# Twelve stack loads issued by ScalarE in place of SyncE, in a fused attention and mixture-of-experts kernel

## What is computed

```python
x = x + _L0_attn_ref(_layernorm(x), w_q, w_k, w_v, w_o)
x = x + _L0_ffn_ref(_layernorm(x), gate_w, w1, w2, w3)
# attention: scores = q k^T / sqrt(16); softmax over the keys; times v; times w_o
# experts: top 2 of softmax(x gate_w^T); silu(x w1^T) * (x w3^T), times w2, weighted and summed
```

## Time and profile before

| | before |
|---|---|
| time, median of 3 runs | 560.6 us (559.58 to 563.26) |
| the profiled execution's own time | 561.26 us |
| its span | 559.4 us |
| TensorE busy in the span | 539.2 us, 96% |
| VectorE busy | 386.4 us, 69% |
| ScalarE busy | 324.4 us, 58% |
| chain of work that ended last | TensorE 81%, VectorE 12%, issue 3% |
| granted TensorE clock, mean | 0.988 |

### The profile page before, as it was taken

One profiled execution on the slowest core, in us unless ns is written; L12 is line 12 of the kernel. 1 busy time (PEld: TensorE's weight loads), 2 busy tenths in 40 slices (PEclk: granted clock), 3 DMA queues, 4 the chain that ended last, 5 costly groups with the idle time before them and its releaser, 6 DMA issues.

```text
span 559.4 us, 9700 instructions
## 1 busy us (share of the span) xinstructions
PE 539.2 (96%) x3508; PEld 392.7 (70%) x3508; DVE 386.4 (69%) x706; ACT 324.4 (58%) x480; POOL 116.2 (21%) x145
## 2 busy tenths in 40 slices
PE   9999999899999999999999999999999999999991
PEld 6887664333333333333778979999999999999981
DVE  6915657889998999961688986755738375667650
ACT  5322116767878777878346463756657475757540
POOL 4300111002022020622001202334341321241212
PEclk9999999989999999999998999999999999999997
DMA  8290367937475753004463599593854757586112
GB/s 325 108 114 0 56 107 88 101 48 88 70 100 73 92 75 99 12 19 166 149 227 119 189 349 346 138 318 50 292 148 159 263 143 279 117 301 160 31 29 37
DMA packets 29068, 78.19 MB, mean 140 GB/s; under 512 B 7644, under 2 KB 8924, under 8 KB 24538
## 3 DMA queue, kind: packets, MB, share of 16 engines
q1 hardware_dynamic: 23722, 68.84, 46.9%
q0 software_dynamic: 5296, 8.69, 8.4%
HBM read 53.11 MB, written 9.32 MB: 112 GB/s over the span
## 4 chain that ended last, share of the span: by engine, by line
PE 81%; DVE 12%; issue 3%; ACT 1%; POOL 1%; DMA 0%; SPq 0%; POOLq 0%; DVEq 0%; ACTq 0%
PE ps L728 16%; PE ps L729 15%; PE ps L730 15%; PE ps_o L740 8%; DVE neg_max L1469 7%; PE ps L759 6%; PE ps L771 4%; PE ps_m L759 3%; PE ps L799 2%; PE ps_m L777 1%; DVE w_lo L1578 1%; PE ps_o L728 1%; PE ps_m L728 1%; PE ps_m L730 1%; PE ps_m L1026 1%
## 5 line engine op out<-in xcount | busy, mean ns | idle before, releaser
L1254 ACT ACTIVATE probs_t<-ps 128x1024 f32<-128x1024 f32 x128 | 124.1, 1021 | 33.2 <-PE ps L771 32.5
L1469 DVE TENSOR_REDUCE neg_max<-ps 128x1 f32<-128x512 f32 x170 | 111.2, 683 | 14.4 <-PE ps L759 10.8
L728 PE MATMUL ps<-xgT_hi,w_hi 128*128 128x256 f32 (+7 forms) x380 | 109.5, 288 | 1.0 <-DVE xgT_lo L1735 1.0
L729 PE MATMUL ps<-xgT_lo,w_hi 128*128 128x256 f32 (+7 forms) x380 | 108.5, 286 | 0.0
L730 PE MATMUL ps<-xgT_hi,w_lo 128*128 128x256 f32 (+7 forms) x380 | 108.5, 286 | 0.0
L728 PEld LDWEIGHTS ps<-xgT_hi,w_hi 128*128 128x128 f32 x380 | 72.0, 189 | 1.3 <-DVE xgT_lo L1735 1.1
L759 PE MATMUL ps<-k_stack,q_stack 48*128 48x512 f32 x170 | 69.3, 462 | 3.5 <-issue 1.7
L729 PEld LDWEIGHTS ps<-xgT_lo,w_hi 128*128 128x128 f32 x380 | 72.0, 189 | 0.1
L730 PEld LDWEIGHTS ps<-xgT_hi,w_lo 128*128 128x128 f32 x380 | 71.9, 189 | 0.0
L740 PE MATMUL ps_o<-probs_t,v_ones 128*32 128x512 f32 x512 | 68.8, 610 | 0.0
L1752 DVE TENSOR_TENSOR act<-gate,ps 128x256 f32<-128x256 f32 (+7 forms) x48 | 20.7, 430 | 66.8 <-PE ps L730 51.2
(11 more groups left out here) (329 smaller groups left out, 983.9 us busy)
## 6 DMA issues: line engine op xcount, KB each, us to landing
w_sb<-w SPq DMA_DIRECT2D x16, 1024.0 KB
w_sb<-w SPq DMA_DIRECT2D x8, 1536.0 KB
w_sb<-w SPq DMA_DIRECT2D x8, 1152.0 KB
q_stack<-q_hi SPq DMA_DIRECT2D x32, 128.0 KB, 5.2
k_stack<-k_hi SPq DMA_DIRECT2D x32, 128.0 KB, 4.9
q_stack<-q_lo SPq DMA_DIRECT2D x16, 128.0 KB, 4.5
k_stack<-k_lo SPq DMA_DIRECT2D x16, 128.0 KB, 5.9
q_hi<-o_raw SPq DMA_DIRECT2D x16, 128.0 KB, 5.1
```

Source lines behind the costliest of these rows:

```text
L728: pe.matmul(o, x_hi, w_hi, start=start, stop=False)
L729: pe.matmul(o, x_hi, w_lo, start=False, stop=False)
L1254: a.activation(probs_t[:, kc % 2, 2 * half:2 * half + 2, :], ps4[:, 2 * (n % 2):2 * (n % 2) + 2, :], ACT.Exp, scale=D ** -0.5).then_inc(s_ ...
L1469: v.tensor_reduce(neg_max[:, g % 2, col:col + 1], max_bank(g, u2), AX.X, ALU.max, negate=True).then_inc(s_mx, 1)
```

## The change: who issues the loads of pair 3, and when

`stack` now takes the engine that issues. SyncE no longer loads pair 3. ScalarE does, in its step (s, p) = (0, 2), after exponentials 2 and 3 of the first group and before exponentials 4 and 5. It waits for the same two semaphores first. The transfers, their sources, their targets and the semaphore that they raise are the same.

```diff
+        def stack(eng, pair, pars, kinds):
+
+            at = pair % RING
+            for par in pars:
+                for part, (qsrc, ksrc) in enumerate(((q_hi, k_hi), (q_lo, k_hi), (q_hi, k_lo))):
+                    dst = slice(HALF * par + D * part, HALF * par + D * (part + 1))
+                    for kind in kinds:
+                        to, frm = (qs, qsrc) if kind == "q" else (ks, ksrc)
+                        eng.dma_start(to[at][dst, :, :].bitcast(f32),
+                                      frm[HALF * par:HALF * (par + 1), pair, :].bitcast(f32)).then_inc(s_stack[at], 16)
...
-                elif s == 0:
-                    ready(3)
-                    stack(3, range(2), "qk")
...
+                if (s, p) == (0, 2):
+                    a.wait_ge(s_ones, RING)
+                    a.wait_ge(s_jd, d_count[n_of["k", 0, 3]])
+                    stack(a, 3, range(2), "qk")
```

More of the change, by code:

```diff
@@ L467, in ready @@
                 sp.wait_ge(s_jd, d_count[n_of["k", pair // HC, pair % HC]])
[L469 to L478, removed]
             for s in range(-4, NG + 2):
@@ L508, in _ @@
                             ready(pair)
-                        stack(pair, [s % 2], "qk")
-                elif s == 0:
-                    ready(3)
-                    stack(3, range(2), "qk")
+                        stack(sp, pair, [s % 2], "qk")
                 elif s == -2:
@@ L515, in _ @@
                     ready(1)
-                    stack(1, range(2), "q")
+                    stack(sp, 1, range(2), "q")
                 elif s == -1:
-                    stack(1, range(2), "k")
+                    stack(sp, 1, range(2), "k")
                     ready(2)
-                    stack(2, range(2), "qk")
+                    stack(sp, 2, range(2), "qk")
                 g = s - 1
```

## The result

The changed kernel takes 569.61 us (median of 6 runs, 565.49 to 573.48); the kernel before, run beside it, takes 561.13 us (median of 6, 559.58 to 565.46). The ratio is 1.0136 with a 95% interval of 1.0098 to 1.0175: slower by 1.4%. The profiled execution took 570.17 us with a span of 568.4, against 561.26 and 559.4 before: 8.9 us more, 9.0 by the spans. Two executions in what follows, one at 573.27 of the burst of six and one at 571.93 of the kernel before, lie over 1.5% above the fastest of their kernel; the medians and the counts take them in, the ratios do not.

A forecast was written before the change was run, and what follows sets the result against it. TensorE, busy for 96% of the span, was taken as the bound, so gains lie only in its idle or low-clock time. -2.6 + 5.9 + 1.2 = +4.5 us, giving 565.2 us, with an 8-in-10 range of 560.4 to 570.

The forecast's parts named there:

- if the clock stays low for much longer than 3.5 us behind the stall: Sign of a wrong forecast: TensorE's stretch at 1.2 GHz behind its wait for ScalarE lasts much longer than 3.5 us.
- dearer issue: Rival: an issue on ScalarE takes 1.0 us, 12.0 us for all in place of 8.2, time 569 us; chance 0.17.
- What is removed, -2.6: At step 8 TensorE no longer waits for the row of group 2, and the slow clock behind goes: -2.6 us.
- ScalarE held for 8.2 us, at 0.60 us an issue: In step 2 the 12 issues, priced by SyncE's rows, keep ScalarE from starting any exponential for 8.2 us.
- with no exponential beside them: Sign of the forecast: between 94 and 102 us no exponential runs beside the 12 issues on ScalarE.
- The stall, +5.9: Exponentials 4 and 5 come late, scores 7 on TensorE 6.1 us late, about 0.2 us comes back: +5.9 us.
- I take the same again, +1.2, and 2.5 as the upper bound.: Low clock of TensorE behind its wait for ScalarE, taken as after the shorter pause: +1.2 us, at most 2.5.
- Not held: Rival: issues cost ScalarE so little that exponential 4 starts at 95.71 as before, time 558.0 us; chance 0.13.
- the row still waits: Rival: ScalarE not held, but the row of group 2 lands as late as before step 8, 560.6 us; chance 0.05.
- Slower by over 1%: Outcome above 566.2 us: the rival at 1.0 us an issue (0.17) and some 0.3 of the forecast (0.19), chance 0.36.

The follow-up runs named there:

- burst of six: The changed kernel with ScalarE issuing 6 of the 12 loads in step 2 and one in each of steps 3 to 8: 567.1 us, 1.006 times before.
- two versions without the burst: Changed kernel with one load on ScalarE in each of steps 2 to 13; kernel before with 6 loads on SyncE in each of rounds 0 and 1: 560.31 us each.
- two halves: The kernel before with pair 3's loads all on SyncE, 6 in round 0 and 6 in round 1 behind the row of group 2: 560.31 us, 0.9954 times before.
- 56 dummies: The changed kernel with 56 dummy matmuls of 128x256 bf16 on TensorE ahead of scores 6: 566.07 us, 1.0047 times before.

## Why the prediction was right, and the term that was not

The time (569.6) lies within 560.4 to 570, near its upper end, above the forecast's own range of 564.4 to 567.9. The mechanism is the forecast's; one term was mis-sized, the clock behind the stall. The prediction had named just this as a sign of being wrong ("if the clock stays low for much longer than 3.5 us behind the stall"), and it came. That 569.6 lies within the range all the same is in part luck: the upper end stood at 570 for the sake of a dearer issue, which didn't come. By its own steps:

- **What is removed, -2.6.** Right. The profile has 2.6, and the two versions without the burst are 2.7 us faster than before. That the row came late because of the twelve loads ahead of it is shown by the two halves; whether by the queue or by the engines isn't.
- **ScalarE held for 8.2 us, at 0.60 us an issue.** Right: 7.99 us from 93.95 to 101.94, 0.62 each. The start, forecast at 94.1 from the end of GpSimd's memset, was 93.95. What the Trainium skill says of the issuing sequencer ("Perfetto Trace Analysis", section "DMA Instruction — HWDGE (DVE, Sync)"), that it is free for its next instruction only when the issue is over, agrees with ScalarE's rows: the next exponential starts 0.44 us after the last issue. The forecast "with no exponential beside them" was wrong in one: exponential 3 went on beside the first issue.
- **The stall, +5.9.** Right: 6.4 in the profile, part of it matmuls at 1.2 GHz. With 56 dummies, at 2.4 GHz throughout, the time is 566.07 - 560.31 = 5.8 us above the halved loads; these are medians from two chips, and by the ratios to before, 1.0047 and 0.9954, it is 5.2. Its profile has pv of step 4 at 106.44, 9.75 us after that of step 3 and 7.05 too many; the long issue (1.78 in place of 0.62) takes 1.16 of them, and 5.9 are left.
- **"I take the same again, +1.2, and 2.5 as the upper bound."** Mis-sized: it was 5.9 us, in a stretch of 17 us of work in place of 3.5. I had one low stretch as a row and took its length as that of all. The runs showed 3.5, 10, 12.3, 16.8, 17, 17.2 and 20.4 us, after gaps of 0.4 to 5.5 us, with no relation to be seen between the gap and the length in these few profiles: 16.8 came after 1.2 us, 3.5 after 1.75. The upper bound should have been open, since no row said what ends such a stretch.
- **The rivals.** The dearer issue (569 by 1.0 us each) gives the right number for a wrong reason; the issue cost what was forecast. "Not held" and "the row still waits" fell with the first issue rows. The Trainium skill's sentence that initiating a transfer usually takes little time beside the transfer itself ("DMA: Bandwidth & Descriptors", section "Issuing engines are not separate DMA queues") agrees with the trace, 0.62 us against 3.7 to 8.9 us to landing, but doesn't decide the time: what counts here is 12 x 0.65 us of issues against the 0.5 us of slack of the exponentials.
- **The chances.** "Slower by over 1%" had 0.36. With the clock term at its measured size the forecast would have been 560.6 - 2.6 + 5.9 + 5.9 = 569.8; the 5.9 of the clock is read from this kernel's own profile, so this is an account and not a second forecast.

## What to carry to other kernels

A transfer's issue cost ScalarE and SyncE some 0.6 us here, and on ScalarE as much for 4 KB as for 128 KB. On an engine that others wait for, one at a time beside a running instruction was free and three fitted, while six or twelve in a row stalled TensorE. A small transfer that is needed soon shouldn't be issued behind large ones that are needed late: splitting the batch around it gave the whole 2.7 us, with no second queue. And where TensorE works close to its bound, price a gap by the stretch at 1.2 GHz that may follow, not by the gap alone: with six in a burst, where TensorE stood still for 1.2 us, eight of eleven executions took some 6 us more than the other three.

## What the runs showed that I had not expected

- The low stretch goes on while TensorE is busy without a gap: 16.80 of 16.80 us after the burst of six, at 4.16 us a step in place of 2.70. What ends it is open. The lengths seen in the attention's first steps and behind the stalls were 3.4 to 20.4 us, and no run here was made to tell what decides them.
- A gap of 0.4 us at step 0 was followed by a low stretch at about 91 us in four of the twelve profiles, of 3.5 or 10 us, and by none in the others. Whether that gap starts it wasn't tested.
- ScalarE issued a transfer in 0.55 us beside an exponential that took its usual 1.02 us.
- The DMA engines served the twelve loads at about the same pace from either queue: the last one issued took 8.9 us at most to land from ScalarE's and 9.2 from SyncE's.
